# Cross attention: the softmax division moves from the transposed head outputs to token rows between two transposes, and the output projection reads two compact blocks

## What is computed

```python
q = _split_heads(Q @ Wq.T + bq)      # Q: layer norm of x
k = _split_heads(K @ Wk.T + bk)      # K, V: the context
v = _split_heads(V @ Wv.T + bv)
scores = jnp.einsum('bhqd,bhkd->bhqk', q, k) / jnp.sqrt(jnp.float32(D_K))
scores = jnp.where(mask[:, None, :, :] == 0, NEG_INF, scores)
attn = jax.nn.softmax(scores, axis=-1)
out = jnp.einsum('bhqk,bhkd->bhqd', attn, v)
out = out.transpose(0, 2, 1, 3).reshape(B, S, H * dk)
return out @ Wo.T + bo
...
x = x + _L1_xattn_ref(_layernorm(x, axis=-1), ctx_1024, ctx_1024, mask_BxSxS2_if1, ...)
```

## Time and profile before

| | us |
|---|---|
| median of 3 runs | 2704.34 |
| lowest and highest | 2702.51, 2709.12 |
| profiled execution, its time | 2702.91 |
| its span | 2701.2 |
| cross attention in it | 1006 to 1728 |
| busy in the whole span: PE, PEld | 2197.2, 1410.5 |
| DVE, ACT, POOL | 1610.9, 902.2, 860.4 |
| TensorE's mean granted clock | 0.942 |

### The profile page before, as it was taken

One profiled execution on the slowest core, in us unless ns is written; L12 is line 12 of the kernel. 1 busy time (PEld: TensorE's weight loads), 2 busy tenths in 40 slices (PEclk: granted clock), 3 DMA queues, 4 the chain that ended last, 5 costly groups with the idle time before them and its releaser, 6 DMA issues. The chain is left out here.

```text
span 2701.2 us, 37571 instructions
## 1 busy us (share of the span) xinstructions
PE 2197.2 (81%) x11892; PEld 1410.5 (52%) x11901; DVE 1610.9 (60%) x2734; ACT 902.2 (33%) x1265; POOL 860.4 (32%) x778
## 2 busy tenths in 40 slices
PE   2340899999999306999999999748999999999998
PEld 1340899999999302333333333534554554554554
DVE  7720454545554453787887888644566566556555
ACT  2410333333333100444554444312233233333332
POOL 0066554425550461222222222111233233233232
PEclk9999999999999756998999899759999999999998
DMA  3262332333322323222222222223323323323322
GB/s 124 74 231 95 113 120 75 111 122 121 112 74 75 109 87 103 68 92 91 90 89 94 69 92 93 95 57 90 80 55 86 79 55 86 79 55 87 78 57 61
DMA packets 149185, 244.82 MB, mean 91 GB/s; under 512 B 22487, under 2 KB 71423, under 8 KB 146811
## 3 DMA queue, kind: packets, MB, share of 16 engines
q1 hardware_dynamic: 107762, 163.65, 21.1%
q0 software_dynamic: 11104, 44.06, 4.8%
q10 hardware_dynamic: 30272, 36.53, 4.2%
HBM read 120.61 MB, written 67.04 MB: 69 GB/s over the span
## 5 line engine op out<-in xcount | busy, mean ns | idle before, releaser
L1087 DVE TENSOR_REDUCE ca_negmax<-ca_na 128x1 f32<-128x512 f32 x544 | 353.7, 677 | 104.4 <-PE ca_na L875 103.1
L1001 ACT ACTIVATE ca_pr<-ca_st 128x1024 f32<-128x1024 f32 x256 | 261.2, 1026 | 268.2 <-PE ca_st L889 268.1
L875 PE MATMUL ca_na<-ca_k_stack,ca_q_stack 64*128 64x512 f32 x544 | 261.1, 519 | 36.4 <-DVE ca_negmax L1087 26.2
L592 DVE TENSOR_TENSOR ex_h<-ex_up,ex_sg 128x512 f32<-128x512 f32 x136 | 94.0, 692 | 307.7 <-ACT ex_sg L555 198.6
L1691 DVE TENSOR_REDUCE sa_negmax<-sa_na 128x1 f32<-128x512 f32 x272 | 182.7, 674 | 131.1 <-PE sa_na L1512 126.9
L515 PE MATMUL ex_gp<-ex_xp,moe_gu_p 128*128 128x256 f32 x1632 | 222.4, 286 | 1.6 <-DVE ex_xp L578 1.4
L889 PE MATMUL ca_st<-ca_q_stack,ca_k_stack 64*128 64x512 f32 x512 | 221.0, 478 | 0.0
L515 PE MATMUL ex_up<-ex_xp,moe_gu_p 128*128 128x256 f32 x1632 | 219.1, 284 | 0.0
L528 PE MATMUL ex_yp<-moe_dn_p,ex_hp 128*128 128x256 f32 x1632 | 209.2, 286 | 11.8 <-DVE ex_hp L582 11.8
L515 PEld LDWEIGHTS ex_gp<-ex_xp,moe_gu_p 128*128 128x128 f32 x1632 | 206.5, 193 | 3.0 <-DVE ex_xp L578 1.8
L528 PEld LDWEIGHTS ex_yp<-moe_dn_p,ex_hp 128*128 128x128 f32 x1632 | 198.9, 191 | 16.0 <-DVE ex_hp L582 15.9
(11 more groups left out here) (258 smaller groups left out, 3993.9 us busy)
## 6 DMA issues: line engine op xcount, KB each, us to landing
sa_q<-sa_qh SPq DMA_DIRECT2D x140, 128.0 KB
sa_k<-sa_kh SPq DMA_DIRECT2D x140, 128.0 KB
ex_raw_m<-masks ACTq DMA_DIRECT2D x34, 512.0 KB, 3.7
moe_gu_raw<-gateupT POOLq DMA_DIRECT2D x8, 2048.0 KB, 8.0
ca_q_stack<-q_parts SPq DMA_DIRECT2D x216, 64.0 KB
ca_k_stack<-k_parts SPq DMA_DIRECT2D x216, 64.0 KB
expert_rows<-rt_zeros SPq DMA_DIRECT2D x20, 512.0 KB, 15.7
k_parts<-ca_kp SPq DMA_DIRECT2D x9, 1024.0 KB, 4.7
```

The source lines that it names most:

```text
L875: pe.matmul(na[s % 2][:, :], q_stack[g][rows, i, t * P:(t + 1) * P], k_stack[g][rows, i, :], start=not masked, stop=True).then_inc(na_full, 1)
L1001: act.activation(pr[:, pair // 2 % 2, h:h + 2, :], st[pair % 2][:, :, :], ACT.Exp, scale=DK ** -0.5).then_inc(exp_done, 1)
L1087: dve.tensor_reduce(negmax[:, g % 2, 1 - s % 2, s // (2 * TB), s // 2 % TB:s // 2 % TB + 1], na[s % 2][:, :], AX.X, ALU.max, negate=True). ...
```

## The change

The division now happens with tokens in the partitions.

- ScalarE still copies `av` to `avs` in slot 6 (`take`), but waits for the transposes of the last `avs`, not for GpSimd.
- A new job `n` in each unit, of four transposes of `avs` into `misc`: there each token has its four heads side by side, each with 16 features and its sum. VectorE takes one reciprocal of 128x16 and multiplies the features into `on[128, 4 tiles, 256]`, a compact row of features for each token.
- Two new jobs `t0`, `t1` in g = 1, of four transposes each of a half of `on`, which ScalarE copies to `outT`, now [128, 2, 512].
- `wo` is now the plain [256, 256] matrix in two blocks, and an output piece has one matmul instead of two.
- The bias `bo` is loaded as a broadcast tile, and GpSimd adds it to x, 128x1024 elements once a row (`add_bias`), after x has been normalised; the addition of `o0` waits for it.
- `invert` and `divide` are gone, with the semaphores `sums_ready` and `outT_ready`.
- `o0` moves from slots 6 to 9 of g = 1 to slots 7 to 10, `v1` from 10 to 13 of g = 2 to 11 to 14.

```diff
-        JOBS = [("m", 0, 0), ("k0", 0, 3), ("k1", 0, 6), ("xT0", 0, 8), ("xT1", 0, 10), ("rv", 0, 12),
-                ("q0", 0, 15), ("m", 1, 0), ("q1", 1, 3), ("o0", 1, 9), ("o1", 1, 15), ("m", 2, 1), ("v0", 2, 7),
-                ("v1", 2, 13), ("m", 3, 1)]
-        PIECES = {"m": 1, "k": 2, "x": 1, "r": 1, "q": 2, "v": 4, "o": 4}
+        JOBS = [("m", 0, 0), ("k0", 0, 3), ("k1", 0, 6), ("xT0", 0, 8), ("xT1", 0, 10), ("n0", 0, 11), ("rv", 0, 12),
+                ("q0", 0, 15), ("m", 1, 0), ("q1", 1, 3), ("t0", 1, 4), ("t1", 1, 6), ("o0", 1, 10), ("n1", 1, 11), ("o1", 1, 15),
+                ("m", 2, 1), ("v0", 2, 7), ("n2", 2, 9), ("v1", 2, 14), ("m", 3, 1), ("n3", 3, 10)]
+        PIECES = {"m": 1, "k": 2, "x": 1, "r": 1, "q": 2, "v": 4, "o": 4, "n": 1, "t": 1}
+        LAST = ["n0", "t0", "t1", "o0", "o1"]
...
@@ output, TensorE @@
                 if piece == 0:
                     bank_free(n)
-                    pe.wait_ge(outT_ready, b * G + 2)
-                t = piece // 2
-                for g in range(2 * (piece % 2), 2 * (piece % 2) + 2):
-                    tok = (2 * c + t) * P
-                    last = pe.matmul(misc[:, t * D:(t + 1) * D], outT[:, g, tok:tok + P], wo[:, g, :],
-                                     start=(g == 0), stop=(g == G - 1))
+                t, i = piece // 2, piece % 2
+                tok = (2 * c + t) * P
+                last = pe.matmul(misc[:, t * D:(t + 1) * D], outT[:, i, tok:tok + P], wo[:, i, :], start=(i == 0), stop=(i == KC - 1))
...
+            def queries(n, u):
+
+                bank_free(n)
+                pe.wait_ge(av_free, u + 1)
+                for t in range(TB):
+                    last = pe.transpose(misc[:, t * P:(t + 1) * P], avs[:, t * P:(t + 1) * P], ident[:, :])
+                last.then_inc(misc_full, 1)
+
+            def features(n, c):
+
+                bank_free(n)
+                for t in range(TB):
+                    last = pe.transpose(misc[:, t * P:(t + 1) * P], on[:, t, c * P:(c + 1) * P], ident[:, :])
+                last.then_inc(misc_full, 1)
...
@@ ScalarE @@
+                elif name[0] == "t":
+                    act.copy(outT[:, c, :], misc[:, :]).then_inc(misc_free, 1)
...
-            def take(u):
+            def take(u, n):
 
                 act.wait_ge(av_done, u * TB + TB)
-                act.wait_ge(outT_ready, u + 1)
+                act.wait_ge(misc_full, n)
                 act.copy(avs[:, :], av[:, :]).then_inc(av_free, 1)
...
@@ GpSimd @@
-            def divide(g, u):
-
-                pool.wait_ge(rec_ready, u * TB + TB)
-                pool.tensor_tensor(outT[:, g, :], avs[:, :], sums[:, :], ALU.mult).then_inc(outT_ready, 1)
+            def add_bias(b):
+
+                pool.wait_ge(xn_ready, b * TB + TB)
+                pool.tensor_tensor(x[:, bass.ds(b * TB, TB), :], x[:, bass.ds(b * TB, TB), :],
+                                   bo[:, :].rearrange("p (a n) -> p a n", a=1).to_broadcast([P, TB, D]), ALU.add).then_inc(bo_added, 1)
...
                     if g == 1:
                         split_q(1, b * nj + (nf + number("q1")), b + 1)
-                        pool.wait_ge(misc_full, b * nj + (nf + number("o1") + 1))
-                    divide((g - 1) % G, u)
+                        add_bias(b)
...
@@ VectorE @@
+                elif name[0] == "n":
+                    heads = misc[:, :].rearrange("p (t h r) -> p t h r", t=TB, r=32)
+                    dve.reciprocal(rec[:, :, :], heads[:, :, :, DK]).then_inc(rec_ready, 1)
+                    dve.wait_ge(rec_ready, a)
+                    dve.tensor_tensor(on[:, :, (c - 1) % G * HG * DK:((c - 1) % G + 1) * HG * DK].rearrange("p t (h d) -> p t h d", d=DK),
+                                      heads[:, :, :, 0:DK],
+                                      rec[:, :, :].rearrange("p t (h a) -> p t h a", a=1).to_broadcast([P, TB, HG, DK]),
+                                      ALU.mult).then_inc(misc_free, 1)
                 else:
+                    dve.wait_ge(bo_added, bx_free)
...
-            def invert(u, i):
-
-                if i == 0:
-                    dve.wait_ge(av_free, u + 1)
-                    dve.memset(tick[:, :], 0.0)
-                    dve.stream_shuffle(sums[:, :], avs[:, :], [DK + i % DK for i in range(32)]).then_inc(sums_ready, 1)
-                    return
-                q = slice((i - 1) * P, i * P)
-                dve.wait_ge(sums_ready, u + 1)
-                dve.reciprocal(sums[:, q], sums[:, q]).then_inc(rec_ready, 1)
```

More of the change, by code:

```diff
@@ L707, in cross_attention @@
         vw = m.sb("vw", [P, G, TB, HG, 32])
-        avs, sums = m.sb("avs", [P, S]), m.sb("sums", [P, S])
-        outT = m.sb("outT", [P, G, S])
-        tick = m.sb("tick", [P, 1])
+        avs, rec = m.sb("avs", [P, S]), m.sb("rec", [P, TB, HG])
+        on = m.sb("on", [P, TB, D])
+        outT = m.sb("outT", [P, KC, S])
         na = [m.ps(f"na{i}", [P, S]) for i in range(2)]
@@ L945, in _ @@
             values(G - 1, TB - 1)
-            for c in range(2):
-                for piece in range(PIECES["o"]):
-                    output(B * nj + nf + c, B, c, piece)
+            for n, name in enumerate(LAST, B * nj + nf):
+                if name[0] == "n":
+                    queries(n, B * G)
+                elif name[0] == "t":
+                    features(n, int(name[1]))
+                else:
+                    for piece in range(PIECES["o"]):
+                        output(n, B, int(name[1]), piece)
         @block.scalar
@@ L1003, in _ @@
                         for n, name in jobs_at(g, s):
-                            if name[0] in "kxm":
+                            if name[0] in "kxmt":
                                 evacuate(b * nj + (nf + n), name, b + 1)
-            take(B * G)
+            take(B * G, B * nj + nf)
+            for n, name in enumerate(LAST, B * nj + nf):
+                if name[0] == "t":
+                    evacuate(n, name, B)
             act.wait_ge(m_in, 64 * (B * G + 1))
@@ L1049, in _ @@
             pool.memset(vw[:, :, :, :, DK:32], 1.0).then_inc(set_up, 1)
-            pool.memset(outT[:, :, :], 0.0).then_inc(outT_ready, 1)
+            pool.memset(on[:, :, :], 0.0).then_inc(bo_added, 1)
             pool.memset(tiny16[:, :], -1.0 / MASKED).then_inc(set_up, 1)
```

52 lines of the change are left out of this document (24 added, 28 removed).

## The result

| | before | after |
|---|---|---|
| median, us | 2704.91 | 2675.25 |
| lowest and highest, us | 2702.51, 2709.12 | 2673.30, 2680.69 |
| ratio, with its 95% interval | | 0.9898 (0.9886 to 0.9911) |
| profiled execution, its time, us | 2702.91 | 2676.99 |
| its span, us | 2701.2 | 2675.3 |

The change makes the kernel 1.0% faster. The medians are 29.7 us apart, the two profiled executions 25.9 us. The 25.9 us have three parts, read from the timelines. The first `take` comes 1.9 us later than before (1088.68 against 1086.77 us): that is the start of the stage. From it to the end of the last values are 600.3 us against 621.4, 21.1 less. From there to the last addition of the stage are 12.6 against 19.35 us, 6.7 less. Behind the stage the two profiles run alike.

The account below looks back on a forecast made before the run. TensorE was taken as the bound, with VectorE close behind. Rows -11, end of the stage -6 and clock -3 make -20 us against the median 2704.3: 2684 us, range 2670 to 2698.

Parts of the forecast that it names:

- A: Most likely case: the forecast as summed, with row sums between -0.7 and -2.5 us, 2675 to 2693 us; chance 0.53.
- rival B: In unit g3 the low clock goes wholly and all 11 us come back: 2676 down to 2665 us; chance 0.24.
- VectorE's lateness: TensorE waits for reductions queued behind reciprocals and shuffle; without these, unit g3 gives -1.5 us a row.
- Transposes against output: On TensorE, six transpose jobs a row at 0.59 us (3.5) cancel eight output pieces shortened by 0.43 us (3.4).
- g0: Unit g0 of a row: shorter first slots and a lost wait against n0 and a bank wait, together +0.2 us.
- g1: Unit g1 of a row: 0.7 us less work, of which the next stack's DMAs allow only -0.5 us.
- g2: Unit g2 of a row: n2 adds 0.59 us against a shortened reduction's wait, together +0.4 us.
- The end of the stage: The last unit's chain, running alone after the last values, gets shorter: -6 us, between -2 and -8.
- The clock: In unit g3, smaller waits leave somewhat fewer stretches at 1.2 GHz: -3 us, bounds 0 and -11.
- Rival C: Hand-overs of the bank misc, each exposed by 0.9 us, eat the row's gain: about 2699 us; chance 0.14.
- D: The clock stays low through g3 in all rows instead of two: slower, 2722 us; chance 0.07.
- E: On TensorE a transpose costs its duration instead of its step: +26 us, 2710 us in all; chance 0.02.

Follow-up runs that it names:

- short operations: Kernel before, with VectorE's shuffle cut to 32 columns and its four reciprocals from 128 columns to 4, all else kept: 2668.59 us.
- doubled transposes: Changed kernel, with each of the 24 new transposes of a row issued twice into the same place: 2691.55 us.
- the earlier copy: Changed kernel, with ScalarE's copy of av into avs in slot 4 instead of 6: 2687.79 us, 0.9919 of before.
- second profile: Changed kernel, unaltered, run once more on the chip of the last two rearranged kernels: 2680.15 us, 0.9887 of before.
- doubled output: Changed kernel, with the first matmul of each output piece's pair issued three times, so a row has 16 output matmuls as before: 2708.51 us.
- the six rearranged ones: Changed kernel with the av copy in slot 4, alone or with moved DMA issues, n3, xT0, xT1, n0 or early stack loads: 2668.23 to 2687.79 us.
- the lateness put back: Changed kernel, with an unused 128-column reciprocal behind the reductions of slots 7, 9, 11, 13 and 15 of g3: 2692.99 us.

## Why the prediction was right, and where it was not

The forecast was 2684 us with a range of 2670 to 2698, faster at 0.77. The result is 2675.25, faster, in the range, and 9 us below the forecast. The range was right, but the most likely case, A, was not what happened: its 2675 to 2693 and rival B's 2665 to 2676 meet at the measured time, and the traces, not the time, tell that the clock did what B says. That the result lies inside A at all, by 0.25 us, is luck. (A's 2693 also holds only if the clock gives nothing; with the -3 it has, a row sum of -0.7 gives 2690.)

- **VectorE's lateness is what the change removes: right, and shown alone.** g3 gave 1.56 us a row (1.5 forecast), g0's first slots 0.68 (0.6). The kernel with short operations shows that nothing else is needed for it. VectorE's groups changed by -149.9 us (reciprocals, shuffles, ticks) and +22.4, so by 127.5, near the 3.8 us a unit; the page's busy time fell by 99 only, because the reductions' mean rose from 677 to 687 ns (5 us) and because time in which two records overlap is counted once there: in this stage that hid 49 us before and 27 after.
- **The evacuation n: right.** 0.25 and 0.43 us, to the hundredth. A reciprocal follows its number of columns.
- **Transposes against output: right as a sum.** The step of 0.59 a job held (1250.34 to 1250.92), 0.43 an output piece too. The figure of about 275 ns (the Trainium skill, "TensorE: Matmul & The Clock Gate", Part 4: PE-mode transpose) is met as a duration, median 273 ns over 132 records here. It is no price here: the doubled transposes cost 0.108 us each.
- **g0: the sum was too low, +0.57 against +0.2.** n0 and the wait of `rv` cost 1.17 (1.1 forecast). The step that failed is "The wait of 0.29 us in slot 10, behind the shuffle, goes". It went, and xT1's wait for xT0's copy, which stands behind four DMA issues of 2.6 us on ScalarE, took its place (0.67 after, 0.65 in the kernel with short operations). I had looked at who ended the wait and not at who would be next.
- **g1: better than forecast, -0.96 with g2's first slots against -0.5.** The stack's DMAs do end last, as I had it, but they allowed more than I had it: from the issue of the last one to the matmul that waits for it are 2.25 us (1277.12 to 1279.37) and not 2.6, and only `score_a` of g2's first slot needs it: its delay of 0.35 us takes the place of m's wait (0.34 before, [0.34 <-DVE all_x L1113] at 1284.24). That the bound is real the earlier copy showed: 0.49 gained in g1, 0.55 lost at g2.
- **g2: right,** +0.36 against +0.4. The sum of the four is -1.59 against -1.4, 12.8 us in all against 11.
- **The end of the stage: right,** -6.7 against -6, and 12.6 us long against 13. It hangs on the clock: in the changed kernel's second profile, with o1 at 1.2 GHz too, it was 14.2 long.
- **The clock: mis-sized, and the largest miss.** -9.5 us against -3. The term that failed is "I expect somewhat fewer low stretches": all of those in g3 and g0, 11.1 us, went, and one of 1.6 us came in the first row. The mechanism is the one of rival B, to which I gave 0.24: without VectorE's lateness the clock doesn't fall in g3 at all. The eleven profiles of kernels without it (after twice, short operations, doubled output, doubled transposes, and the six rearranged ones) have no stretch below full clock in a g3 or the g0 behind it; the two with it (before, and the lateness put back) both do. They are one execution each, and the two differ in how often it fell. My argument against B, that 3.31 us groups keep an inner wait of 0.33, was wrong as a reason: that wait stays and the clock holds. Which of the two lost waits it was, that of slots 12 to 15 or that of slots 0 to 2, was not separated.
- Rival C (the bank takes VectorE's place) holds in kind, not in size: four waits for the bank and the one for `take`, 0.2 to 0.5 us each, are 1.9 us a row together. Since the transposes (six times 0.59) and the output's saving (eight times 0.43) cancel, these waits, less those whose place they took, are what is left to explain why the change gives 1.6 us a row where the short operations give 2.8. D and E did not occur.
- The sum once more: the forecast was -20, the medians differ by 29.7. The clock is 6.5 us of the difference, the rows 1.1 and the end of the stage 0.7. Against it stand 1.9 us by which the first `take` came late in this profile, and 0.5 in the first row. The medians differ by 3.8 us more than the profiled executions do. This I can't assign.

## What to carry to other kernels

Ask of every wait that a change removes who would be waited for next: here a DMA issue on ScalarE stood right behind the shuffle, and the stack's DMAs right behind TensorE's work. A cheap probe for it is to shrink the suspected operation in place and keep all else; it showed in one run that the rearrangement paid 1.2 us a row for a gain of 2.8. When an engine that issues DMAs also evacuates a shared bank, place the issues behind the evacuation unit by unit, and issue early the part of a load that doesn't depend on the late operand.
